# GpSimd's scatter calls of the second half in pairs, each pair behind TensorE's signals

## The reference

```python
logits = x @ gate_w
top_val = jnp.max(logits, axis=-1, keepdims=True)
top_id = jnp.argmax(logits, axis=-1)
xs = x * jax.nn.sigmoid(top_val)
g = jnp.einsum('th,ehi->eti', xs, rt_gate)      # 128 -> 256
u = jnp.einsum('th,ehi->eti', xs, rt_up)        # 128 -> 256
y = jnp.einsum('eti,eih->eth', jax.nn.silu(g) * u, rt_down)   # 256 -> 128
routed = jnp.einsum('eth,te->th', y, jax.nn.one_hot(top_id, E))
```

## Time and profile before

| | before |
|---|---|
| median of three runs | 837.2 us (835.5 to 839.71) |
| the profiled execution's own time | 840.62 us |
| its span, first to last instruction | 837.4 us |
| TensorE busy | 785.9 us (94%) |
| VectorE busy | 650.4 us (78%) |
| ScalarE busy | 558.8 us (67%) |
| GpSimd busy | 251.1 us (30%) |
| 16 DMA engines, queue 1 (SyncE's) / queue 0 (GpSimd's) | 17.6% / 3.5% of the span |
| mean granted clock of TensorE | 0.98 of full speed |

### The profile page before, as it was taken

One profiled execution on the slowest core, in us unless ns is written; L12 is line 12 of the kernel. 1 busy time (PEld: TensorE's weight loads), 2 busy tenths in 40 slices (PEclk: granted clock), 3 DMA queues, 4 the chain that ended last, 5 costly groups with the idle time before them and its releaser, 6 DMA issues.

```text
span 837.4 us, 15003 instructions
## 1 busy us (share of the span) xinstructions
PE 785.9 (94%) x4424; PEld 635.5 (76%) x4464; DVE 650.4 (78%) x1730; ACT 558.8 (67%) x1007; POOL 251.1 (30%) x293
## 2 busy tenths in 40 slices
PE   5899997897878899999999999999999999999997
PEld 4788776776768899967777777777777777777775
DVE  5888889887824467778888888888888888888774
ACT  3577667685524434467777778678777777877765
POOL 2332322666265225112321331242133133211000
PEclk9999999999879899999999999999999999999999
DMA  6337784562523334100000000000000000000000
GB/s 170 87 112 197 200 238 135 165 176 72 161 85 105 92 110 115 51 25 11 26 27 0 25 25 0 25 25 19 6 25 25 0 25 25 16 11 13 13 1 25
DMA packets 91175, 55.79 MB, mean 67 GB/s; under 512 B 13439, under 2 KB 87799, under 8 KB 90999
## 3 DMA queue, kind: packets, MB, share of 16 engines
q1 hardware_dynamic: 75440, 41.29, 17.6%
q0 software_dynamic: 4096, 8.40, 3.5%
q10 hardware_dynamic: 11591, 5.50, 2.4%
HBM read 32.23 MB, written 22.94 MB: 66 GB/s over the span
## 4 chain that ended last, share of the span: by engine, by line
PE 76%; DVE 10%; ACT 7%; issue 4%; another core or an unknown queue 2%; DMA 0%; DVEq 0%; ACTq 0%; SPq 0%
PE PS L870 7%; PE PS L1124 7%; PE PS L855 7%; PE PS L1146 7%; PE PS L1148 7%; PE PS L1147 6%; PE PS L1126 6%; PE PS L1125 6%; PE PS L1068 4%; PE PS L1135 4%; PE PS L878 3%; PE PS L1133 2%; PE PS L1051 2%; PE PS L1036 2%; DVE xn L1205 2%
## 5 line engine op out<-in xcount | busy, mean ns | idle before, releaser
L812 ACT ACTIVATE sil<-PS,b_in_c 128x512 f32<-128x512 f32 x256 | 162.2, 685 | 92.2 <-PE PS L1133 60.7
L1591 DVE TENSOR_TENSOR sil_l<-sil,sil_h 128x512 fp32r<-128x512 f32 x256 | 164.8, 686 | 48.5 <-ACT sil_h L820 48.5
L542 POOL TENSOR_TENSOR ve<-mv,eps 128x4 f32<-128x4 f32 x64 | 19.7, 309 | 444.1 <-DVE mv L1199 442.6
L820 ACT ACTIVATE sil_h<-sil 128x512 fp32r<-128x512 f32 x224 | 128.9, 631 | 0.0
L1146 PE MATMUL PS<-sil_h,wout_l 128*128 128x512 f32 x256 | 118.8, 464 | 1.7 <-DVE sil_l L1591 1.6
L1124 PE MATMUL PS<-x4T_h,win_l 128*128 128x512 f32 x256 | 102.4, 400 | 0.9 <-ACT sil L812 0.4
L1148 PE MATMUL PS<-sil_h,wout_h 128*128 128x512 f32 x256 | 100.6, 393 | 0.0
L1147 PE MATMUL PS<-sil_l,wout_h 128*128 128x512 f32 x256 | 100.2, 391 | 0.0
L1126 PE MATMUL PS<-x4T_h,win_h 128*128 128x512 f32 x256 | 100.0, 391 | 0.0
L1125 PE MATMUL PS<-x4T_l,win_h 128*128 128x512 f32 x256 | 99.9, 390 | 0.0
L1575 DVE TENSOR_SCALAR dec<-PS,b_in_c 128x512 bf16<-128x512 f32 x128 | 95.4, 745 | 3.9 <-PE PS L1126 2.1
(11 more groups left out here) (174 smaller groups left out, 1575.1 us busy)
## 6 DMA issues: line engine op xcount, KB each, us to landing
x_sorted<-zeros SPq DMA_DIRECT2D x4, 1280.0 KB, 6.8
xs_in<-x_sorted SPq DMA_DIRECT2D x20, 256.0 KB
y_sorted<-yo ACTq DMA_DIRECT2D x18, 256.0 KB
X<-in_x SPq DMA_DIRECT2D x16, 256.0 KB
rows<-xn SPq DMA_DIRECT2D x16, 256.0 KB
out<-res SPq DMA_DIRECT2D x16, 256.0 KB
ctxT<-in_ctx_t SPq DMA_DIRECT2D x16, 240.0 KB
ctx_rows<-in_ctx_kv SPq DMA_DIRECT2D x16, 240.0 KB
```

The lines of the kernel that those rows point to most:

```text
L812: act.activation(tile(sil[p % 2], c, W), bank(2 * (p % 2) + c), ACT.Silu, bias=b_in_c[:, 2 * p + c:2 * p + c + 1]).then_inc(t_silu, 1)
L820: act.activation(tile(sil_h[p % 2], c, W), tile(sil[p % 2], c, W), ACT.Copy).then_inc(t_hi, 1)
L1591: dve.tensor_tensor(tile(sil_l[p % 2], c, W), tile(sil[p % 2], c, W), tile(sil_h[p % 2], c, W).bitcast(F32), ALU.subtract).then_inc(t_lo, 1)
```

## The change

Two things change in GpSimd's program, and nothing in that of another engine.

`scatter` waits for its group's scaling only in the first call of a group (t % 4 = 0), in both halves. The other three calls of the group stand behind that one on the same engine.

The 32 calls of the second half go in 16 pairs, and a new function `behind_tensor(n)` stands ahead of each. It waits until gate and up signal n has arrived, turn signal n // 2 + 1, and, for n above 3, down signal n - 3. For the pairs 0 to 15 the number n is 3, 3, 4, 5, 6, 7, 8, 9, 10, 10, 11, 12, 13, 14, 15, 16.

```diff
-                if h:
-                    pool.wait_ge(k_late, k - HG + 1)
-                elif k:
-                    pool.wait_ge(k_act, k)
-                else:
-                    pool.wait_ge(k_scaled, 1)
+                if t % G == 0:
+                    if h:
+                        pool.wait_ge(k_late, k - HG + 1)
+                    elif k:
+                        pool.wait_ge(k_act, k)
+                    else:
+                        pool.wait_ge(k_scaled, 1)
                 pool.sem_inc(pool_passed, 1)
                 pool.indirect_dma_start(...)
...
+            def behind_tensor(n):
+
+                pool.wait_ge(r_gu_ps, n)
+                pool.wait_ge(r_xT_ps, n // 2 + 1)
+                if n > 3:
+                    pool.wait_ge(r_y_ps, n - 3)
+
             pool.wait_ge(placed, 2)
-            for t in range(B0[1], B):
-                scatter(t, 1, NG)
+            for i in range(HBS[1] // 2):
+                behind_tensor(3 + 7 * i // 8)
+                for t in (B0[1] + 2 * i, B0[1] + 2 * i + 1):
+                    scatter(t, 1, NG)
```

## The result

The changed kernel takes 828.7 us (median of four, 827.52 to 829.43); the kernel before, in the same comparison, 838.37 us (four, 835.5 to 839.71). The ratio is 0.9897, interval 0.9869 to 0.9924: faster by 9.7 us. The prediction had 820.3, a gain of 16.9 us from 837.2: the direction came out and the time lies in the range (816 to 833), but the gain is only a little over half of the one forecast (8.5 us counted from 837.2). Two executions far out of line, 1111.52 us at a granted clock of 0.656 in experiment 15 and 2745.84 us of the kernel before in the comparison of experiments 13 and 14, count as slow and are in none of the ratios.

What follows compares the result with a forecast made beforehand. TensorE, busy for 94% of the span, was taken as the bound, with two routed-stage stalls to gain: 19.4 - 1.5 - 1.0 = 16.9 us, so the median would go from 837.2 to 820.3 us, range 816 to 833.

Steps and rivals of the forecast that it cites:

- the two stalls: TensorE in the routed stage, 231.3 to 246.9 and 267 to 280 us: together they cost 19.4 us, low clock included.
- Long runs of scatters hold the signals: GpSimd's runs of 12 and 8 scatters delay TensorE's signals, which arrive within about 1 us of a run's end.
- By the runs of four above, late signals then cost TensorE nothing: Routed stage: with later runs at most four, no TensorE loss, as in 246.9 to 267, busy 20.0 of 20.1 us.
- (1): GpSimd's waits: 48 dropped and 46 added cost nothing; without the cover of its slower engine, 0.79 us a pair.
- Lock: Rival, chance 0.04: each second-half pair is held for both VectorE copies, 3.8 us behind its signal; 823.5 us.
- (2): Second-half scatters: pairs of 2.24 us against signals every 2.9, so single pairs; starting run of six costs 1.5 us.
- (3): Second half's end: last scatter ends 269.0, load 274.6, unit 10 wanted 274.5; no slack, 1.0 us for late signals.
- 19.4 - 1.5 - 1.0 = 16.9: Routed stage gain in us: both stalls, less the starting run of six, less signals late at a pair.
- one stall stays: Rival, chance 0.14: six scatters at the start suffice for the first stall, only the second goes; 828.4 us.
- Slower: Rival, chance 0.08: even two scatters hold TensorE's signals until landed, 5.9 us a signal; 850.9 us.
- Nothing gained: Rival, chance 0.08: late signals come from instruction supply or memory, not GpSimd's runs; 837 us.
- The prediction's own sign of being wrong: Routed stage: dribbling matmuls still there, unit 10's turn waiting over 3 us for its load, or pair pitch over 4.6 us.

Runs made afterwards that it cites:

- experiment 15: Kernel before without the second half's 32 scatters, on a chip where the kernel before takes 838.84 us: 820.03 us, ratio 0.9763.
- 13: Kernel before with eight added HBM-to-HBM copies of 1 MB in rows of 512 bytes: 844.36 us against 843.34, ratio 1.0034.
- 14: Kernel before with eight added HBM-to-HBM copies of 2 MB in large pieces: 843.78 us against 843.34, ratio 1.0013.
- experiment 17: Kernel before, dropped group waits, 1.1 us GpSimd operation behind every fourth scatter, no wait for TensorE, on a late chip: 828.87 us, ratio 0.9873.
- experiment 1: Kernel before with only the waits for scaling dropped except in a group's first call, no waits for TensorE: 815.43 us against 815.62, ratio 1.0000.
- experiment 18: Kernel before with only the waits for scaling dropped except in a group's first call, on a late chip: 842.7 us, ratio 1.0007.
- experiment 5: The changed kernel itself, on a chip without late signals: 815.72 us against 815.78 for the kernel before, ratio 1.0004.
- 8: Kernel before, dropped group waits, GpSimd operation of about 1.1 us behind every fourth scatter, no wait for TensorE, chip without late signals: 825.55 us, ratio 1.0116.
- 9: Kernel before with eight added 512 KB HBM-to-HBM copies in the routed stage, chip without late signals: 815.6 us, ratio 1.0002.
- 10: Changed kernel with eight added 512 KB HBM-to-HBM copies in the routed stage, chip without late signals: 816.6 us, ratio 1.0014.
- 11: Changed kernel with each group's second pair also waiting until the group before has landed, chip without late signals: 815.21 us, ratio 0.9998.
- 2: Changed kernel with pairs waiting for the gate and up signal alone, chip without late signals: 816.79 us against 815.62 for the kernel before, ratio 1.0015.
- experiment 3: Kernel before, dropped group waits, a one-column memset on GpSimd behind each pair, no wait for TensorE, chip without late signals: 815.63 us, ratio 1.0003.
- 7: Kernel before without the second half's 32 scatters, chip without late signals, a repeat: 815.5 us, ratio 0.9994.
- 4: Kernel before without the second half's 32 scatters and the waits for their landing, chip without late signals: 815.55 us, ratio 0.9994.
- 12: Kernel before without the second half's 32 scatters, on another chip without late signals: 816.09 us, ratio 1.0005.
- experiment 16: Changed kernel with each group's second pair also waiting until the group before has landed, on a late chip: 831.09 us, ratio 0.9882.

## Why the prediction was right in direction and wrong in its second step and in size

- **TensorE is the bound, and the two stalls are what can be gained.** Right, and shown: without the scatters a late chip gains 18.8 us (experiment 15), and the gain of the change, 9.7, is near that of its span (11.2) and of the turns (59.9 to 49.65, 10.3).
- **Long runs of scatters hold the signals.** Shown by experiment 15, and by 17 for the length of a run. Two readings under it were wrong. "Within about 1 us of its end" does not fit the copy at 241.20, 2.9 us ahead of the run's end at 244.06. And "By the runs of four above, late signals then cost TensorE nothing" took too few rows: in the next run of four before, 254.17 to 258.96, a turn that ends at 256.88 + 0.60 = 257.48 is answered 2.5 us late, and experiment 17 shows what runs of four cost, some 4 us.

```profile
256.88 0.60 PE L855 MATMUL PS<-WA,xs_in 128*128 128x128 f32 x4
260.00 0.60 ACT L649 ACTIVATE xsT<-PS 128x512 f32<-128x512 f32 x1 [0.88 <-remote]
```

- **(1) The dropped and added waits cost nothing.** Right: the dropped ones by experiments 1 and 18, the added ones by experiment 5, where the scatters keep their pitch. The rule of the Trainium skill that was weighed there (SBUF — State Buffer, section "Who interferes with whom") did not decide the time. In the trace after, the scatters took 996, 980 and 989 ns on the mean, by source buffer, and the one at 242.62, which began during two copies that VectorE ran from 241.91 to 242.87, took 1.08 us. No scatter of the second half took over 1.10 us there, against up to 1.21 before and 1.29 in experiment 17 (265.47, beside copies from 265.09 to 265.85). "Lock", the rival built on that rule, is out: pairs 7 and 8 started 0.8 us behind their signals and took 2.25 and 2.30 us.
- **(2) "Pairs come singly with a pause", and "No run is then longer than six at the start and four later".** This is the step that failed, and it fails by the prediction's own numbers, before any late signal. The sixteen pairs are released by signals 3 to 16: 13 signals of 2.9 us, 37.7 us, stand against 15 pairs at the scatters' own pitch of 2 x 1.28 = 2.56, 38.4 us. The step set the length of one pair, 2.24, against the distance of two signals, and forgot that pairs which share a signal leave the next pair behind its own. By the prediction pair 3 starts at 237.3; pair 4 is then due at 239.9 and its signal 6 at 234.14 + 2.9 = 237.0 (238.5 with the 1.5 us that TensorE is pushed back), so it has nothing to wait for. Experiment 5 shows it undisturbed: two runs of 16. On the late chip three runs were of six, and each ended at a pair whose signal came late.
- **What the runs cost.** From turn to turn, against 5.79 us a unit: the first run of six cost 1.3 us (233.13 to 240.22), near the 1.5 of the prediction. The second run, with the half clock behind it, cost 4.4 (240.22 to 256.24), where the prediction had none. The units from there to 282.78 cost 3.4, where it had 1.0, with bounds 0 and 3, for pairs that get their signal late.
- **(3) The last scatter meets unit 10's need.** The last scatter ended at 278.29 instead of 269.0, since signal 16 was sent at 272.25 + 1.95 = 274.20 and not at 266.0, and this cost nothing of its own: unit 10 is turned at 282.78 without waiting. The danger is real: experiments 8 and 17 paid 7.1 and 3.6 us for it. Where no signal is late the end came near the forecast (264.5, against 263.1 when the prediction's 269.0 is counted from unit 3's turn, 228.11 there), but by GpSimd's own pitch and not by the signals. The 2.9 us from the end of a scatter to the load behind it is not one number: it was 1.4 here (278.29 to 279.7), and 1.4 in experiment 1 (266.06 to 267.48).
- **The sum.** 19.4 - 1.5 - 1.0 = 16.9 should have read 19.4 - 1.3 - 4.4 - 3.4 = 10.3. Of the rivals, "one stall stays" gave 828.4. That this lies beside the measured 828.7 is luck: the six scatters at the start cost 1.3 us and not the first stall, and what was lost came with the later runs. "Slower" needed that each pair hold its signals until its landing. The pair of 250.76 did not (a down product that ends at 251.94 is answered at 252.05); the pair of 269.74 to 272.02 did, once (the product that ends at 268.14 + 1.95 = 270.09 is answered at 272.72). "Nothing gained" is what happens on a chip without late signals, for a reason that no row of the trace before could tell.
- **The prediction's own sign of being wrong** was there: the stretch from 231.3 to 247 still has 107 matmuls where 143 belong, with pauses of "issue".

Why the pairs' waits help at all follows from the same rows, though no run tests it alone: a run can't go past a pair whose signal is late, so a late signal itself ends the run that holds it, after 2 to 6 scatters and not after 8 or 12.

What stays open: why some chips hold TensorE's signals under a run of scatters and others do not. More traffic of this core is excluded (9, 10, 13, 14), and the scatters are necessary (15) but not sufficient (1). What path in such a chip they share with a signal, no run here shows, nor whether it is the chip itself or work of other cores on it; only the chip of experiments 1 to 11 was measured at three different times, with medians of 815.6 to 815.8 us for the kernel before. Which of the three counters the pairs must wait for was only tried where none is late (2). It was not tried either to let each pair wait for a signal of its own, so that the gate is slower than the scatters and pairs of two stay apart.

## What to carry to other kernels

A wait for another engine's signals spaces work out only if the signals come more slowly than the work goes by itself. So set the pitch of the whole gated sequence against that of its signals (38.4 against 37.7 us here), and not one piece against one signal; a piece that starts behind its signal finds the next ones there. If gaps are wanted, put something of a fixed length between the pieces and measure that it makes a gap (1.0 us did in experiment 17, 0.12 us did not in experiment 3). Then look how far the end of the spaced work is from its first reader, since TensorE waited for what lay past that point (7.1 and 3.6 us). Before a stall that the profile calls "remote" is worked on, the kernel is to be run on a second chip: the whole gain here existed on some chips only.

## What the runs showed of the hardware

- The same program takes 815.6 and 815.5 us on two chips and 838.4, 838.8 and 843.3 on three others, 2.8% or more apart; the three late ones overlap in their single runs. Of the 23 us between 815.6 and 838.8, some 19 are the routed stage's stalls under the scatters. With the scatters left out (experiment 15) a late chip still takes 820.0, 4.5 more, and unit 1 is turned 2.0 to 3.6 us later (222.03 against 220.04, 218.73 and 218.48 in experiments 7, 4 and 12), so part of it lies ahead of the routed stage; its cause was not looked for.
- On late chips the signals were late, at a pitch of 1.27 us between scatters, by 7 to 11.5 us under runs of 12 (before and experiment 18), by 3.3 to 5.0 under runs of six (after and experiment 16), by up to 2.6 under runs of four (experiment 17), and once by 2.6 under a run of two that stood 0.8 us behind a run of four (after, 272.72). On the others a run of 32 gave none over 0.3 us late.
- While a signal is late TensorE is slow itself: nine matmuls of a product start after 0.84 us of "issue" (after, 236.50), and one wait is 2.2 us of "issue" (experiment 16), with nothing that they waited for in the profile.
